# First attention with the keys on the partitions and a rough pass for the maxima, W1 loaded in each expert stage, latent rows placed in two parts

## The chip, the cores and the metric

The kernel runs on one NeuronCore of a Trainium2 chip, as one program. The metric is the device time of one execution in microseconds; the figure of a version is the median of its runs. The engines are TensorE (PE), VectorE (DVE), ScalarE (ACT), GpSimd (POOL) and SyncE (SP, here only the engine that issues transfers). They run side by side and wait for each other by semaphores only.

## The reference

Two sequences of 1024 tokens with 256 values each, all in float32. Six blocks follow each other, each added to x after a layer norm:

```python
x = x + 0.5 * moe(layernorm(x))                  # 16 experts, top 2, 256 -> 512 -> 256, silu
x = x + attention(layernorm(x))                  # 16 heads of 16: see below
x = x + 0.5 * moe(layernorm(x))                  # the same weights again
x = x + 0.5 * lora_ffn(layernorm(x))
x = x + latent_attention(layernorm(x))           # 16 heads, 64 rotary values, latents of 48 and 64
x = x + 0.5 * lora_ffn(layernorm(x))
```

The first attention is the one that the change rewrites:

```python
scores = einsum('bthd,bshd->bhts', q, k) * tril(ones((T, T)))
attn = softmax(scores / T ** 0.5, axis=-1)
out = einsum('bhts,bshd->bthd', attn, v).reshape(B, T, H * Dh)
return out @ Wo
```

The mask multiplies: a later key has the score 0, not minus infinity, and so the weight exp(0 - max). Its part of the result is exp(-max) times the sum of all later values, and the kernel, which computes no scores of later keys, adds that part by itself.

## The kernel before, in words

The stages run one after the other on one core: load, experts 0, first attention, experts 1, a small stage of experts with low rank (lora), the latent attention (mla), lora again, store. x stays in SBUF throughout. Each stage is a block in which every engine has its own list of instructions; nothing is scheduled by a planner, so the order of the work on an engine is the order in which its code is written, and where engines must meet a semaphore is waited for.

**First attention** (`attention_stage`, lines 538 to 1003). A group is 4 heads of one sequence; there are 4 groups in each of 2 sequences, in loops of the hardware. Rows of x are normalised, transposed on PE (L678), and projected by Wqkv (L689) for one group at a time, 8 tiles of 128 tokens. To keep float32 accuracy in one fast pass, the queries and keys are split in a high and a low part (rounded to fp32r, and the rest), which lie side by side in rows QS and KS; PE transposes them (L699) into QT and KT, in 64 rows for each head, so that one matmul with all 128 rows gives high times high, high times low and low times high. A unit is one tile of 128 queries and one head, 32 units in a group. For each: scores with the queries on the partitions (L719), the maximum of each row on DVE (L921, L922 with the mask on the diagonal, L933 for its negative), the exponential on ACT with the negative maximum as the bias of each partition (L850), then a transpose of each 128x128 tile of probabilities on PE (L730), a copy of it from PSUM by ACT (L869), and the values (L740, float32, four heads in four column tiles of 32). An extra column of ones in the values gives the denominator. The parts of later keys come from L750 and L751 (tiles of sums that POOL makes), the rows of the result from DVE (L951 to L967), and after each sequence the output projection (L794, L807). Probabilities of the next units and the projections of the next group are written between, by the tables `steps` and `ahead`.

**Experts** (`moe_stage`). The weights W1 (16 experts, 8.4 MB) and W2 (8.4 MB) lie in SBUF. W1 is loaded once, in experts 0 (L253), and stays there through the first attention; W2 is loaded in both. The normalised rows XN, too, have one place for the experts and, in between, for the attention's rows. PE waits for both weights and then works through the slots of the experts.

**Latent attention** (`mla_stage`). It works on pairs of heads, 8 in each sequence. In a pair PE writes rough scores (L1490, 512 columns each) for the maxima that DVE takes (L1759), then scores with the keys on the partitions (L1509, three passes of high and low parts), the exponentials on ACT (L1648), the values (L1518). The rows of queries and keys of the next pair are projected (L1458, L1465) meanwhile: ACT writes the high parts SH (L1623), DVE the low parts SL (L1753), and SP moves them to their partitions in QH, QL, KH and KL by transfers from SBUF to SBUF, eight for the rotary rows (L1360) and four for the latent ones (L1364), for each half of the tokens. That is `placed`:

```python
def placed(it, buf, half):
    sp.wait_ge(s_hi.handle, s_hi.at(6 * it + 3 * half + 2))
    sp.wait_ge(s_lo.handle, s_lo.at(6 * it + 3 * half + 2))
    for src, q, k in ((SH, QH, KH), (SL, QL, KL)):
        ...
```

POOL fills QH, QL, KH and KL once (L1386, L1390).

## Time and profile before

| | us |
|---|---|
| median of 3 runs | 2616.44 |
| lowest, highest | 2613.11, 2621.42 |
| profiled execution, its own time | 2618.63 |
| its span in the profile | 2616.8 |
| mean granted clock of PE | 0.909 |
| first attention, from its first instruction to its last | 346.5 to 886.9 |
| experts 0 | 18.0 to some 346 |
| experts 1 | 887.1 to some 1215 |
| latent attention | some 1272 to 2540 |

The profile comes from one execution. Times in the timeline count from the start of the span. A matmul's own duration says little about the rate of PE, since matmuls overlap: the step from one start to the next does. The granted clock is a share of full speed (2.4 GHz), so 0.50 is 1.2 GHz.

### The profile page before, as it was taken

The page shows a single profiled execution, that of the slowest core. Times are in us where ns is not written, and L with a number is a line of the kernel's source. Part 1 is how long each engine was busy: PE and PEld are TensorE (multiplying, and loading weights), DVE is VectorE, ACT ScalarE, POOL GpSimd, SP SyncE. Part 2 cuts the span into 40 slices and gives each one's busy share as a digit, 9 for nine tenths or more (in the row PEclk, how much of TensorE's full clock was granted, in tenths as well). Part 3 has the DMA queues.
Part 4 walks back from the last instruction along what each step waited for, and adds up shares of the span by engine and source line. Part 5 has one row for each costly group of instructions (what it writes and reads, how often), then busy time and mean ns, then how long its engine had stood idle before and what let it go on. Part 6 is the DMA issues. An engine that isn't in the chain of part 4 may idle for free. (4 is left out here: it accounts for less than half of the span.)

```text
span 2616.8 us, 40985 instructions
## 1 busy us (share of the span) xinstructions
PE 2141.2 (82%) x11352; PEld 1398.8 (53%) x11353; DVE 1407.2 (54%) x3614; ACT 979.4 (37%) x2011; POOL 755.6 (29%) x480
## 2 busy tenths in 40 slices
PE   4699549997889859972559999999876999999986
PEld 4466336666666646652435555555463555555455
DVE  5222267785778632226445666666335666666525
ACT  1122148885888412212223333333311333333322
POOL 3100320000000130015204555555601555555531
PEclk9999869998999769996758999999976999999998
DMA  7321210000000331222232222212003122112101
GB/s 319 115 62 60 73 40 2 2 2 2 2 2 2 148 109 58 62 62 59 82 73 49 49 49 48 48 45 48 3 12 80 43 49 48 44 47 48 42 1 43
DMA packets 80101, 139.49 MB, mean 53 GB/s; under 512 B 13136, under 2 KB 47440, under 8 KB 78160
## 3 DMA queue, kind: packets, MB, share of 16 engines
q1 hardware_dynamic: 57680, 106.21, 14.6%
q0 software_dynamic: 6144, 16.79, 2.0%
q10 hardware_dynamic: 16128, 14.69, 1.7%
q8 instruction: 72, 1.18, 0.2%
q14 instruction: 77, 0.63, 0.1%
HBM read 60.95 MB, written 27.39 MB: 34 GB/s over the span
## 5 line engine op out<-in xcount | busy, mean ns | idle before, releaser
L1410 POOL TENSOR_TENSOR mla_PS<-mla_PS,mla_PT 128x1024 f32<-128x1024 f32 x192 | 457.4, 2382 | 269.7 <-ACT mla_PT L1648 266.9
L1759 DVE TENSOR_REDUCE mla_MXP<-PS 128x1 f32<-128x512 f32 x512 | 342.4, 689 | 308.0 <-PE PS L1490 303.7
L1648 ACT ACTIVATE mla_PT<-PS 128x1024 f32<-128x1024 f32 x256 | 262.5, 1025 | 467.4 <-PE PS L1509 465.2
L1490 PE MATMUL PS<-mla_KH,mla_QH 128*128 128x512 f32 x512 | 226.7, 484 | 75.1 <-DMA mla_KL<-mla_SL 61.8
L1518 PE MATMUL PS<-mla_PT,mla_CN 128*64 128x512 f32 x1024 | 284.7, 635 | 0.4 <-ACT mla_PT L1648 0.4
L380 DVE COPY moe_HT<-PS 128x512 f32<-128x512 f32 x96 | 66.4, 692 | 319.5 <-PE PS L505 313.4
L1490 PEld LDWEIGHTS PS<-mla_KH,mla_QH 128*128 128x128 f32 x512 | 96.6, 206 | 253.6 <-DVE mla_MXP L1759 133.3
L1509 PE MATMUL PS<-mla_QH,mla_KH 128*128 128x512 f32 x512 | 215.4, 421 | 0.5 <-ACT mla_QH L1635 0.5
L850 ACT ACTIVATE att_PR<-PS,att_NB 128x128 f32<-128x128 f32 (+7 forms) x256 | 193.4, 756 | 53.5 <-DVE att_NB L933 46.8
L1509 PE MATMUL PS<-mla_QL,mla_KH 128*128 128x512 f32 x512 | 205.5, 401 | 0.0
L1509 PE MATMUL PS<-mla_QH,mla_KL 128*128 128x512 f32 x512 | 204.4, 399 | 0.0
L730 PE MATMUL PS<-C,att_PR 128*128 128x128 f32 x1152 | 174.2, 278 | 10.4 <-ACT att_PR L850 6.1
L499 PE MATMUL PS<-W,moe_ST 128*128 x384 | 177.1, 605 | 2.7 <-issue 1.5
L869 ACT COPY att_PT<-PS 128x512 f32<-128x512 f32 (+3 forms) x384 | 173.0, 494 | 11.3 <-PE PS L730 10.6
L513 PE MATMUL PS<-moe_W,moe_HT 128*128 x768 | 173.7, 379 | 0.0
L533 POOL DMA_INDIRECT XN<-slots_out,moe_PO x32 | 32.8, 1026 | 453.5 <-DMA slots_out<-moe_YS 444.3
L921 DVE TENSOR_REDUCE att_MY<-PS 128x1 f32<-128x128 f32 (+6 forms) x224 | 153.4, 685 | 13.0 <-PE PS L719 10.6
L730 PEld LDWEIGHTS PS<-C,att_PR 128*128 128x128 f32 x1152 | 133.4, 141 | 44.6 <-ACT att_PT L869 18.1
L1771 DVE RECIPROCAL PS<-PS 128x128 f32<-128x128 f32 x128 | 108.7, 917 | 79.7 <-PE PS L1525 79.7
L513 PEld LDWEIGHTS PS<-moe_W,moe_HT 128*128 128x128 f32 x768 | 142.2, 190 | 17.3
L719 PE MATMUL PS<-att_KT,att_QT 128*128 128x512 f32 (+1 forms) x384 | 138.6, 423 | 11.5 <-DVE att_KT L903 5.6
L1410 POOL TENSOR_TENSOR mla_PS<-mla_PT 128x1024 f32<-128x1024 f32 x32 | 75.7, 2367 | 248.9 <-ACT mla_PT L1648 248.9
(263 smaller groups left out, 3514.7 us busy)
## 6 DMA issues: line engine op xcount, KB each, us to landing
moe_W<-in_W_dram SPq DMA_DIRECT2D x8, 2048.0 KB, 25.7
moe_XS<-slots_in SPq DMA_DIRECT2D x100, 128.0 KB, 2.0
slots_out<-moe_YS ACTq DMA_DIRECT2D x96, 128.0 KB, 1.7
W<-in_W_dram SPq DMA_DIRECT2D x4, 2048.0 KB, 14.6
mla_QH<-mla_SH SPq DMA_DIRECT2D x64, 128.0 KB, 2.5
mla_KH<-mla_SH SPq DMA_DIRECT2D x64, 128.0 KB, 2.4
mla_QL<-mla_SL SPq DMA_DIRECT2D x64, 128.0 KB, 2.5
mla_KL<-mla_SL SPq DMA_DIRECT2D x64, 128.0 KB, 2.4
```

Source lines behind the costliest of these rows:

```text
L499: ins = pe.matmul(bank(2 + u)[:, :], ST[:, u, k, :], g.W1[:, experts[u], k, :], start=(k == 0), stop=(k == KD - 1))
L513: ins = pe.matmul(bank(6 + u)[:, 0:D], HT[:, u, k, :], W2[:, experts[u], k, :], start=(k == 0), stop=(k == KF - 1))
L730: ins = pe.transpose(bank(4 + c % 2)[:, k * P:(k + 1) * P], PR[:, n % 2, (k0 + k) * P:(k0 + k + 1) * P], ident)
L850: act.activation(PR[:, n % 2, 0:w], scores(n, w), ACT.Exp, bias=NB[:, n:n + 1], scale=SEQ ** -0.5).then_inc(s_p.handle, 1)
L869: act.copy(PT[:, i % 2, h, k0:k0 + nk, :], bank(4 + c % 2)[:, 0:nk * P].rearrange("p (k s) -> p k s", s=P)).then_inc(s_ptc.handle, 1)
L921: dve.tensor_reduce(MY[:, n:n + 1], scores(n, w)[:, 0:i * P], AX_X, ALU.max).then_inc(s_mx.handle, 1)
L1410: pool.tensor_tensor(PS[:, :], PT[:, slot(0), :] if k == 1 else PS[:, :], PT[:, slot(k), :], ALU.add).then_inc(s_ps.handle, 1)
L1490: pe.matmul(bank(piece_bank(n))[:, :], QH[:, buf, h, tile * P:(tile + 1) * P], KH[:, buf, h, c * HB:(c + 1) * HB], start=True, stop=True). ...
L1509: ins = pe.matmul(bank(st_bank(s, h))[:, :], kk[:, buf, h, ks], qq[:, buf, h, qs], start=(n == 0), stop=(n == 2))
L1518: ins = pe.matmul(bank(6)[h * DKVL:(h + 1) * DKVL, :], CN[:, k, 0:DKVL], PT[:, slot(k), h * HB:(h + 1) * HB], start=(k == 0), stop=(k == T ...
L1648: act.activation(PT[:, slot(k), :], banks(st_bank(s, 0), 2)[:, :], ACT.Exp, scale=MLA_SCALE).then_inc(s_p.handle, 1)
L1759: dve.tensor_reduce(MXP[:, n // NPC, c, h, t:t + 1], bank(piece_bank(n))[:, :], AX_X, ALU.max).then_inc(s_mx.handle, 1)
```

## The change

The first attention is written anew, all eight groups one after another without loops of the hardware, in 24 slots for each.

- Queries and keys are projected for a group of four heads and 512 tokens at once (L759, now with the weights as the stationary operand), so that they come out with the heads on the partitions. ACT writes the high parts SH, DVE the low parts SL, and SP moves 16 rows at a time into QT and KT: 24 transfers a group. Row 32 of each head's 64 rows holds the maximum in QT and -1 in KT.
- A rough pass (L774, 32 of the 64 rows, which leave out the low parts of the queries; the mask is added by L777) writes scores with the queries on the partitions in 40 pieces a group; DVE reduces each. The maxima of four tiles are transposed on PE (L785), and ACT copies four single rows into QT.
- The scores proper (L799, 64 rows, with L803 for the mask) have the keys on the partitions and the maximum already subtracted, so the exponential needs no bias and its result goes into the values (L815) without a transpose. The result is copied (ACT), transposed back for four tiles (L823) and finished by DVE and POOL.
- Rows, values and later parts of the second sequence, and the output projection of the first, are written into slots of the loop, through bank 7.
- W1 and XN have a place of their own in each expert stage, and W1 is loaded in both.
- `placed` waits for the high parts, issues their transfers, and then waits for the low parts, for the rotary and for the latent rows.
- Names of semaphores for the loading and storing of x are merged, the constants get nine more columns, Wqkv is split into Wqk and Wv, and the order of the host's arrays follows.

```diff
-                    if rep == 0:
-                        sp.dma_start(g.W1[:, e:e + 4], dram["W1"][:, e:e + 4]).then_inc(g.s_w1.handle, 16)
+                    sp.dma_start(g.W1[:, e:e + 4], dram["W1"][:, e:e + 4]).then_inc(s_w1.handle, 16)
...
-                    def scores_of(it, n, buf, free):
-                        if n == 0:
-                            pe.wait_ge(s_kc.handle, s_kc.at(TB * (it + 1)))
-                        if not free:
-                            pe.wait_ge(s_p.handle, s_p.at(NU * it + scores_read_before(n)))
-                        i, h = n // HG, n % HG
-                        width = (i // 2 + 1) * 2 * P
-                        for c in range(0, width, 512):
-                            w = min(512, width - c)
-                            ins = pe.matmul(bank(sc_bank(n) + c // 512)[:, 0:w], QT[:, h // 2, h % 2, i * P:(i + 1) * P],
-                                            KT[:, buf, h // 2, c:c + w], start=True, stop=True)
-                        ins.then_inc(s_sc.handle, 1)
...
-                    def probs_transposes(it, n, first):
-                        pe.wait_ge(s_p.handle, s_p.at(NU * it + n + 1))
-                        for c in range(first_chunk[n], first_chunk[n + 1]):
-                            _, k0, nk = chunks[c]
-                            if c >= 2 or not first:
-                                pe.wait_ge(s_ptc.handle, s_ptc.at(NC * it + c - 1))
-                            for k in range(nk):
-                                ins = pe.transpose(bank(4 + c % 2)[:, k * P:(k + 1) * P], PR[:, n % 2, (k0 + k) * P:(k0 + k + 1) * P], ident)
-                            ins.then_inc(s_ptp.handle, 1)
...
+                sp.wait_ge(s_fill.handle, s_fill.at(5))
+                for G in range(NG):
+                    if G >= 2:
+                        sp.wait_ge(s_st.handle, s_st.at(NSL * (G - 1)))
+                    for src, s_made, rows in ((SH, s_hi, ((QT, 0, 0), (KT, 64, 0), (QT, 0, 16), (KT, 64, 33))), (SL, s_lo, ((KT, 64, 16), (QT, 0, 33)))):
+                        sp.wait_ge(s_made.handle, s_made.at(2 * (G + 1)))
+                        for h in range(HG):
+                            for dst, at, row in rows:
+                                to = 64 * (h % 2) + row
+                                sp.dma_start(f32(dst[to:to + DH0, G % 2, h // 2, :]), src[at + DH0 * h:at + DH0 * (h + 1), :]).then_inc(s_rows.handle, 16)
+                sp.wait_ge(s_w.handle, s_w.at(48))
...
+                pool.memset(f32(QT[:, :, :, :]), 0.0).then_inc(s_fill.handle, 1)
+                pool.memset(f32(KT[:, :, :, :]), 0.0).then_inc(s_fill.handle, 1)
+                pool.memset(MB[:, :], 0.0).then_inc(s_fill.handle, 1)
+                pool.wait_ge(s_fill.handle, s_fill.at(3))
+                for h in range(2):
+                    pool.memset(f32(KT[64 * h + 32:64 * h + 33, :, :, :]), -1.0).then_inc(s_fill.handle, 1)
+                    pool.wait_ge(s_fill.handle, s_fill.at(4 + h))
+                pool.memset(VV[:, :, :], 0.0).then_inc(s_fill.handle, 1)
+                pool.wait_ge(s_fill.handle, s_fill.at(6))
+                pool.memset(VV[:, :, :].rearrange("p t (h d) -> p (t h) d", d=VW)[:, :, DH0:DH0 + 1], 1.0).then_inc(s_fill.handle, 1)
+
...
+                def rough_scores(H, ns):
+                    for n in ns:
+                        q, t, _, k0, w, hs = pieces[n]
+                        if n == 0:
+                            pe.wait_ge(s_rows.handle, s_rows.at(NROW * (H + 1)))
+                        if NPC * H + n >= 2:
+                            pe.wait_ge(s_mx.handle, s_mx.at(NPC * H + n - 1))
+                        i = 4 * q + t
+                        diag = k0 + w == (i + 1) * P
+                        out = bank(n % 2)[:, 0:len(hs) * w].rearrange("p (h k) -> p h k", k=w)
+                        for m, h in enumerate(hs):
+                            row = slice(64 * (h % 2), 64 * (h % 2) + 32)
+                            ins = pe.matmul(out[:, m, :], QT[row, H % 2, h // 2, i * P:(i + 1) * P], KT[row, H % 2, h // 2, k0:k0 + w], start=(m == 0),
+                                            stop=(not diag and m == len(hs) - 1))
+                        if diag:
+                            ins = pe.matmul(out[:, :, w - P:w], IDR[:, :], bcast(NQ[:, :], 1, len(hs)), start=False, stop=True)
+                        ins.then_inc(s_sh.handle, 1)
...
+                def max_rows(G, q):
+                    n = 2 * G + q
+                    misc(s_nm, 4 * (n + 1))
+                    pe.wait_ge(s_mb.handle, s_mb.at(n + 1))
+                    for t in range(4):
+                        ins = pe.transpose(MISC[:, t * P:(t + 1) * P], MB[:, t:t + P], ident)
+                    ins.then_inc(s_mt.handle, 1)
...
+                def scores_of(G, s):
+                    q, j = key_of(s // 2)
+                    pair = s % 2
+                    if s in (0, TB):
+                        pe.wait_ge(s_nm.handle, s_nm.at(4 * (2 * G + q + 1)))
+                    if NSL * G + s >= 2:
+                        pe.wait_ge(s_p.handle, s_p.at(NSL * G + s - 1))
+                    c0 = columns(q, j)
+                    diag = j >= 4 * q
+                    for hh in range(2):
+                        row = slice(64 * hh, 64 * hh + 64)
+                        ins = pe.matmul(st_banks(s)[:, hh, c0:HB], KT[row, G % 2, pair, j * P:(j + 1) * P], QT[row, G % 2, pair, q * HB + c0:(q + 1) * HB],
+                                        start=True, stop=not diag)
+                    if diag:
+                        for hh in range(2):
+                            ins = pe.matmul(st_banks(s)[:, hh, c0:c0 + P], IDR[:, :], NK[:, :], start=False, stop=True)
+                    ins.then_inc(s_st.handle, 1)
...
+                def values_of(G, kk):
+                    q, j = key_of(kk)
+                    pe.wait_ge(s_p.handle, s_p.at(NSL * G + 2 * kk + 2))
+                    if j == 0:
+                        pe.wait_ge(s_oc.handle, s_oc.at(2 * G + q))
+                    c0 = columns(q, j)
+                    tile, last = TB * (G // NG0) + j, 4 * q + 3
+                    for h in range(HG):
+                        hv = (G % NG0 * HG + h) * VW
+                        ins = pe.matmul(bank(6)[h * VW:(h + 1) * VW, c0:HB], VV[:, tile, hv:hv + VW], PT[:, kk % 2, h, c0:HB], start=(j == 0), stop=(j == last))
+                    ins.then_inc(s_v.handle, 1)
...
+                rough_scores(0, range(NPC0))
+                max_rows(0, 0)
+                rough_scores(0, range(NPC0, begin[0]))
+
+                for G in range(NG):
+                    for s in range(NSL):
+                        H, todo = pieces_at(G, s)
+                        scores_of(G, s)
+                        if s == 6:
+                            max_rows(G, 1)
+                        if s == 17 and G + 1 < NG:
+                            max_rows(G + 1, 0)
+                        rough_scores(H, todo[:1])
+                        if s % 2 == 0 and (s or G):
+                            values_of(G if s else G - 1, s // 2 - 1 if s else NKEY - 1)
+                        rough_scores(H, todo[1:])
+                        if (G, s) in filler:
+                            fill(*filler[G, s])
+                        if s == 4 and G:
+                            out_transposes(G - 1, 1)
+                        if s == 11:
+                            out_transposes(G, 0)
+                        if projected_at(G, s):
+                            K, half = projected_at(G, s)
+                            misc(s_lo, 2 * K + half + 1)
+                            projections(K, half, MISC)
+                values_of(NG - 1, NKEY - 1)
+                out_transposes(NG - 1, 1)
+                for i in range(TB + 1):
...
+                act.wait_ge(s_fill.handle, s_fill.at(7))
...
+                def max_copies(G, q):
+                    n = 2 * G + q
+                    act.wait_ge(s_mt.handle, s_mt.at(n + 1))
+                    for h in range(HG):
+                        row = 64 * (h % 2) + 32
+                        act.copy(QT[row:row + 1, G % 2, h // 2, q * HB:(q + 1) * HB], MISC[VW * h:VW * h + 1, :]).then_inc(s_nm.handle, 1)
...
+                def maxima(H, ns):
+                    for n in ns:
+                        q, t, c, k0, w, hs = pieces[n]
+                        dve.wait_ge(s_sh.handle, s_sh.at(NPC * H + n + 1))
+                        out = MX[:, q, c, hs[0]:hs[-1] + 1:2, t]
+                        dve.tensor_reduce(out, bank(n % 2)[:, 0:len(hs) * w].rearrange("p (h k) -> p h k", k=w), AX_X, ALU.max).then_inc(s_mx.handle, 1)
...
                     def placed(it, buf, half):
                         tok = slice(half * HB, (half + 1) * HB)
-                        sp.wait_ge(s_hi.handle, s_hi.at(6 * it + 3 * half + 2))
-                        sp.wait_ge(s_lo.handle, s_lo.at(6 * it + 3 * half + 2))
-                        for src, q, k in ((SH, QH, KH), (SL, QL, KL)):
+                        for src, q, k, s_made in ((SH, QH, KH, s_hi), (SL, QL, KL, s_lo)):
+                            sp.wait_ge(s_made.handle, s_made.at(6 * it + 3 * half + 2))
                             for h in range(2):
                                 for m, dst in enumerate((q, k)):
                                     i = 32 * (2 * m + h)
                                     sp.dma_start(f32(dst[ROT, buf, h, tok]), src[i:i + 32, 0:2, :]).then_inc(s_kr.handle, 16)
-                        sp.wait_ge(s_lo.handle, s_lo.at(6 * it + 3 * half + 3))
-                        for src, k in ((SH, KH), (SL, KL)):
+                        for src, k, s_made in ((SH, KH, s_hi), (SL, KL, s_lo)):
+                            sp.wait_ge(s_made.handle, s_made.at(6 * it + 3 * half + 3))
                             for h in range(2):
                                 sp.dma_start(f32(k[LAT, buf, h, tok]), src[h * 64:h * 64 + DQL, 2, :]).then_inc(s_kl.handle, 16)
 
@@ -1841,7 +1940,7 @@
 
 
```


**Order of the instructions.** On PE, in the main loop of a group before (L719 scores, L730 transposes of probabilities, L699 transposes of queries and keys, L740 values):

```order
L719 MATMUL PS<-att_KT,att_QT 128x512 [waits att_probs]
L719 MATMUL PS<-att_KT,att_QT 128x256
L728 REGISTER_ALU [waits att_probs]
L730 MATMUL PS<-C,att_PR 128x128 [waits att_probsT_copied]
L730 MATMUL PS<-C,att_PR 128x128 x3
L728 REGISTER_ALU
L730 MATMUL PS<-C,att_PR 128x128 [waits att_probsT_copied]
L694 ISA
L699 MATMUL PS<-C,att_QS 128x128 [waits att_low_parts]
L699 MATMUL PS<-C,att_QS 128x128
L699 MATMUL PS<-C,att_KS 128x128 x2
L740 MATMUL PS<-att_PT,att_VV 32x128 [waits att_out_sum,att_probsT_copied]
```


And now on PE, in slots 17 and 18 of the first group (L799 scores, L803 masks, L785 the rows of maxima, L774 rough scores, L815 values):

```order
L799 MATMUL PS<-att_QT,att_KT 128x512 [waits att_probs]
L799 MATMUL PS<-att_QT,att_KT 128x512
L803 MATMUL PS<-att_NK,att_IDR 128x128 x2
L785 MATMUL PS<-C,att_MB 128x128 [waits att_block_max,att_xnT_copied]
L785 MATMUL PS<-C,att_MB 128x128 x3
L774 MATMUL PS<-att_KT,att_QT 128x512 [waits att_piece_max] x2
L799 MATMUL PS<-att_QT,att_KT 128x384 [waits att_probs]
L799 MATMUL PS<-att_QT,att_KT 128x384
L803 MATMUL PS<-att_NK,att_IDR 128x128 x2
L774 MATMUL PS<-att_KT,att_QT 128x512 [waits att_piece_max]
L815 MATMUL PS<-att_PT,att_VV 32x512 [waits att_probs]
L815 MATMUL PS<-att_PT,att_VV 32x512 x3
```


The runs of equal instructions are gone: between two sets of scores PE now changes from tiles of 64 rows to 128, to 32, to column tiles of 32, and back. Before, only the values had a tile of their own.

On SP, in the latent attention, the transfers of half a pair before:

```order
L1360 DMA mla_QH<-mla_SH 64x1x512 [waits mla_low_parts,mla_high_parts]
L1360 DMA mla_KH<-mla_SH 64x1x512
L1360 DMA mla_QH<-mla_SH 64x1x512
L1360 DMA mla_KH<-mla_SH 64x1x512
L1360 DMA mla_QL<-mla_SL 64x1x512
L1360 DMA mla_KL<-mla_SL 64x1x512
L1360 DMA mla_QL<-mla_SL 64x1x512
L1360 DMA mla_KL<-mla_SL 64x1x512
L1361 REGISTER_ALU
L1364 DMA mla_KH<-mla_SH 48x512 [waits mla_low_parts]
L1364 DMA mla_KH<-mla_SH 48x512
L1364 DMA mla_KL<-mla_SL 48x512 x2
```


And now:

```order
L1459 DMA mla_QH<-mla_SH 64x1x512 [waits mla_high_parts]
L1459 DMA mla_KH<-mla_SH 64x1x512
L1459 DMA mla_QH<-mla_SH 64x1x512
L1459 DMA mla_KH<-mla_SH 64x1x512
L1459 DMA mla_QL<-mla_SL 64x1x512 [waits mla_low_parts]
L1459 DMA mla_KL<-mla_SL 64x1x512
L1459 DMA mla_QL<-mla_SL 64x1x512
L1459 DMA mla_KL<-mla_SL 64x1x512
L1461 REGISTER_ALU
L1463 DMA mla_KH<-mla_SH 48x512 [waits mla_high_parts]
L1463 DMA mla_KH<-mla_SH 48x512
L1463 DMA mla_KL<-mla_SL 48x512 [waits mla_low_parts]
```


The wait for the low parts moved from ahead of the first transfer to ahead of the fifth, and in the latent rows from the first to the third.

## Rows read from the trace of the kernel before

**Rows 1.** Windows: us, each engine's busy time (instructions), granted clock, DMA share, GB/s.

```profile
346.50:886.90 540.40, 472.78 (x4656) 356.09 (x4656) 403.90 (x1561) 418.24 (x1051) 27.34 (x52) 0.97 0.01 4
```

**Rows 2.** The page's costliest groups, three of the attention's.

```profile
L850 ACT ACTIVATE att_PR<-PS,att_NB 128x128 f32<-128x128 f32 (+7 forms) x256 | 193.4, 756 | 53.5 <-DVE att_NB L933 46.8
...
L730 PE MATMUL PS<-C,att_PR 128*128 128x128 f32 x1152 | 174.2, 278 | 10.4 <-ACT att_PR L850 6.1
...
L869 ACT COPY att_PT<-PS 128x512 f32<-128x512 f32 (+3 forms) x384 | 173.0, 494 | 11.3 <-PE PS L730 10.6
```

**Rows 3.** The page's group of L1490, its idle time and what ended it.

```profile
L1490 PE MATMUL PS<-mla_KH,mla_QH 128*128 128x512 f32 x512 | 226.7, 484 | 75.1 <-DMA mla_KL<-mla_SL 61.8
```

**Rows 4.** Timeline of PE in one pair of the latent attention: start, us.

```profile
1547.41 1.03 PE L1518 MATMUL PS<-mla_PT,mla_CN 128*64 128x512 f32 x4
1548.37 0.50 PE L1509 MATMUL PS<-mla_QH,mla_KH 128*128 128x512 f32 x1
...
1549.62 0.40 PE L1509 MATMUL PS<-mla_QH,mla_KL 128*128 128x512 f32 x1
1553.01 0.49 PE L1490 MATMUL PS<-mla_KH,mla_QH 128*128 128x512 f32 x1 [2.99 <-DMA mla_KL<-mla_SL]
```

**Rows 5.** Timeline of ACT, DVE and SP in the same pair.

```profile
1539.68 1.07 ACT L1623 CAST mla_SH<-PS 128x512 fp32r<-128x512 f32 x2
...
1542.27 1.27 DVE L1753 TENSOR_TENSOR mla_SL<-PS,mla_SH 128x512 fp32r<-128x512 f32 x2
...
1543.63 0.60 SPq L1360 DMA_DIRECT2D mla_QH<-mla_SH  x1
...
1548.11 0.60 SPq L1360 DMA_DIRECT2D mla_KL<-mla_SL  x1
1548.81 1.17 SPq L1364 DMA_DIRECT2D mla_KH<-mla_SH  x2
1550.03 1.23 SPq L1364 DMA_DIRECT2D mla_KL<-mla_SL  x2
```

**Rows 6.** Windows of PE alone: us, busy, granted clock, DMA share, GB/s.

```profile
1554.50:1557.50 3.00, 3.00 (x9) 0.50 0.00 0
1749.60:1756.20 6.60, 6.58 (x16) 0.54 0.00 0
```

**Rows 7.** Windows of the experts: both weight loads, then W2 alone.

```profile
18.00:81.00 63.00, 29.94 (x136) 27.84 (x136) 29.66 (x153) 11.17 (x25) 31.68 (x32) 1.00 0.91 367
887.00:947.00 60.00, 29.92 (x136) 27.84 (x136) 29.75 (x153) 11.17 (x25) 31.35 (x32) 0.51 0.65 246
```

**Rows 8.** Timeline of PE, tiles of 128 rows, then of 64.

```profile
1590.73 0.39 PE L1509 MATMUL PS<-mla_QH,mla_KL 128*128 128x512 f32 x1
1590.95 0.40 PE L1490 MATMUL PS<-mla_KH,mla_QH 128*128 128x512 f32 x1
1591.28 0.50 PE L1465 MATMUL PS<-mla_CTH,mla_GH 64*128 64x512 f32 x1
1591.62 0.39 PE L1465 MATMUL PS<-mla_CTL,mla_GH 64*128 64x512 f32 x1
1591.86 0.39 PE L1465 MATMUL PS<-mla_CTH,mla_GL 64*128 64x512 f32 x1
```

**Rows 9.** The page's groups of a float32 matmul and of a reduce.

```profile
L1759 DVE TENSOR_REDUCE mla_MXP<-PS 128x1 f32<-128x512 f32 x512 | 342.4, 689 | 308.0 <-PE PS L1490 303.7
...
L499 PE MATMUL PS<-W,moe_ST 128*128 x384 | 177.1, 605 | 2.7 <-issue 1.5
```

**Rows 10.** Groups by shape: copies of one row, memsets.

```profile
L1635 ACT CAST mla_QH<-PS 1x512 fp32r<-1x512 f32 x64 | 36.8, 575 | 102.6 <-PE PS L1497 101.8
...
L650 POOL MEMSET att_QT<- 128x4096 f32 x1 | 3.5, 3515 | 0.0
...
L1390 POOL MEMSET mla_KL<- 1x4096 f32 x1 | 3.5, 3502 | 0.1
```

**Rows 11.** Timeline of ACT: the first exponential.

```profile
372.66 0.37 ACT L850 ACTIVATE att_PR<-PS,att_NB 128x128 f32<-128x128 f32 x1 [2.19 <-DVE att_NB L933]
```

760 lines of the change are left out of this document (391 added, 369 removed).

## The prediction

> **What bounds the kernel now.** I read the windows by stage first, then the page's costliest groups, then the timeline where PE idles. In the first attention, 346.5 to 886.9, PE is busy 472.8 of 540.4 us at a granted clock of 0.97 [rows 1]. Less some 80 us of beginnings and ends, that is eight groups of heads of 57.6 us each. ACT is busy 418 us and DVE 404 [rows 1]. So PE bounds it, with ACT and DVE not far behind (by their shares, 45 and 43 us of a group). Three groups show what the layout costs: 193.4 us of exponentials and 173.0 us of copies on ACT, and 1152 transposes of probabilities on PE, 174.2 us [rows 2]. The latent attention is bound by PE too, but has a hole in each pair of heads: L1490 sat idle 75.1 us, 61.8 of them until transfers into mla_KL had landed [rows 3]. One case: PE's last matmul starts at 1549.62 and the next at 1553.01 [rows 4]. The SL half was complete on DVE at 1543.54, SP issued its first transfer at 1543.63 although ACT had finished the SH half at 1540.75, and the last of 12 issues ended at 1551.26 [rows 5]. After the hole the granted clock is 0.50 for some 3 us, in 4 of 14 cases 0.54 over 6.6 us [rows 6]. A matmul that takes 0.23 us takes 0.43 there.
>
> **Latent attention.** The total work stays; four SH transfers go before the wait for SL. SP then issues them at about 1540.8 to 1543.4 (pitch 0.64, from 1543.63 to 1548.11 for eight [rows 5]), the SL four from 1543.6 to 1546.2, the latent four to 1548.7. The last landed 1.75 us after its issue ended before (1551.26 to 1553.01), so now at about 1550.4, against 1550.0 where PE runs dry: a hole of 0.4 instead of 3.0 us. What is late next is nothing on SP: its following wait is one pair later. The 14 holes sum to 44.8 us, and the two beginnings of a sequence make up the rest of the 61.8; 2.6 us each is 36. Without a hole the clock should stay up: ten falls of 1.7 us and four of 3.4 are 30 us [rows 6]; I count 28. The two beginnings of a sequence (8.5 us of idle each) save 1.7 each, 3.4. Sum -68 us. Ends: -45 if half the falls stay, -80 if the holes close fully and the clock's loss was larger. I take the value for a hole below 0.5 us, since the landing time is a measured difference.
>
> **W1 again.** Four loads of 2048 KB return to the second experts stage. The first one, with both loads, took 63.0 us from its start to the first slot load, the second, with W2 only, 59.6; DMA share is 0.91 against 0.65 there [rows 7], so the extra 8.4 MB lie beside the router's work mostly. +3.4 us (0 to +6). The merged semaphores of x and the nine more columns of constants cost nothing: they touch the two ends of the program, where one wait takes the place of another.
>
> **First attention.** PE loses the transposes of probabilities, of QS and KS, and gains rough scores and masks. Counted from the order of the program, for all 8 groups, at full clock: an F32R pass over 512 columns starts every 0.23 us [rows 8], one of 384, 256, 128 columns 0.17, 0.11 and 0.11 (no row shows 128 columns alone; between 0.06, a quarter of 0.23, and 0.151, L730's 174.2/1152 [rows 2], which holds waits too). A float32 matmul is two passes, for 512 columns of 0.43 to 0.46 us each (177.1/384 at most [rows 9]).
> - Rough scores L774: 384 matmuls, 192 of 512, 64 of each other width: 69.5 us. Scores L799: the same, 69.5.
> - Masks L777 192 and L803 256: 20.5 + 27.4.
> - Values L815, 96 sets of four column tiles of 32, 48 sets over 512 columns; L1518's pair of column tiles, four passes, gives 0.96 to the next start with one change of tile in it, 0.85 without [rows 4]; 61.9.
> - Projections L759 27.3, transposes (192) 21, values, later values and output L740, L748, L751, L835 41.
>
> Sum 338. The two matmuls of a scores pair lie on different 64 rows. Whether they run together no row shows (L1465 uses the same 64 rows and its passes follow at 0.24 [rows 8]); between 0 and -42 I take -20.
> **Changes of tile size** are what the new order is full of: 920 (to 128 rows 359, to 32 rows 273, to 64 rows 192, to column tiles 96) against some 350 before. From 128 to 64 rows the next start is 0.33 us later instead of 0.23, and the one after that 0.34 too [rows 8]: 0.10 to 0.21 a change. By TensorEngine Tiling (Array Packing) of the Trainium skill, section Key Properties, changing the tiling mode drains TensorE; the trace agrees, 0.10 us or more. The same counting gives 57.6 us for a group of before with 0.175 a change, which is what the trace has, so 0.175: 161 us. PE needs 338 - 20 + 161 = 479 us.
> Of that about 30 us lie in the prologue and 9 in the tail; the loop is 440, 55 a group. Four us a group I add for waits: at slot 6 ACT copies four rows of maxima, 4 x 0.575 = 2.3 us [rows 10], and the scores of slot 8 wait for them, with ACT's full exponentials (1.03 us each) queued behind; DVE's reduces (40 a group, up to 0.69 each [rows 9]) sum to 24 us and hide. Loop 472.
> **Prologue.** ACT now waits for seven fills on POOL before its first copy: two of 4096 elements at 3.5, two of one row at 3.5 (one partition costs what 128 do), one of 8192, 7, and small ones [rows 10]: 22.8 us, to 369.4 (before, the first copy ran at 354.6). Rows, values and projections take to 382, two low parts and 24 transfers at 0.64 (15.4) to 399, 26 rough pieces through DVE with the maxima between to 416.5: 70 us, against 26 before (346.5 to 372.7 [rows 11]). The second sequence has no prologue of its own now; its rows and values are filled into slots of the loop, counted above. The tail is 13. Whole stage 70 + 472 + 13 = 555 against 540: **+15 us**. Ends: -95 and +85, from the price of a change and of a pair, below.
>
> **Sum.** -68 + 3.4 + 15 = -50 us against the profiled execution's 2618.6, which is 2.2 above the median 2616.4: **2569 us**. ACT and DVE, 45 and 43 us of a group before, come to about 28 and 30, which buys nothing as long as PE is the bound.
>
> **Rivals.** (a) *Changes of tile are cheap and pairs run together.* At 0.10 a change, -69, and another -22 for scores and rough pieces on different rows: attention 464, total 2478. For it: L1518's two column tiles do overlap, four passes of 0.43 in 0.96 [rows 4]. Against it: both the 0.33 and the 0.34 are there for one change [rows 8]. The page TensorE: Matmul & The Clock Gate of the Trainium skill, its section on small K, says that matmuls on different row groups run concurrently, starting within 4 ns of each other; no row here shows it for rows. By that rule alone the pairs would give the other -22 and a total of 2547.
> (b) *The change of tile decides, on the slow side.* Place: PE between each rough piece, its mask, the scores and the values. If a change costs 0.25, as where drain, exposed weight load and restart add (0.10 + 0.11 + some), 920 x 0.075 = +69: attention 624, total 2638, slower than before. It decides from about 0.24 a change. For: the second 0.34. Against: the group of before, calibrated at 0.175.
> (c) *The hole stays.* If another transfer or DVE's low part ends the wait, and the clock falls all the same, MLA gives 20 and not 68: total 2617, no change. Against: SP is idle before 1543.6, ACT's part is ready 2.9 us before [rows 5].
>
> **Numbers.** Forecast case (2530 to 2605) 0.52; (a) 0.19, of it half above 2500; (b) 0.17; (c) 0.12, two thirds within the bound. 0.3%, 8 us, is about what a measurement of this kernel can tell. Faster by more: 0.52 + 0.19 + 0.03 + 0.01 from (b)'s lower end = 0.75; same 0.08; slower 0.17. Range 2495 to 2630; it leaves out (a)'s cheaper half and (b)'s dearer half.
>
> **What would show it.** In the new profile: the idle time of L1490's successor near 15 us instead of 75, and the clock of a pair's start at 1.00; the starts of a scores matmul after a rough mask 0.30 to 0.40 us after that mask; PE busy over 85% of a group of 59 us; the first exponential 70 us after the stage's start; ACT's busy share in the stage about half. A group of under 50 us says (a), one over 65 says (b). Holes of 3 us in the latent attention say (c). I would be wrong altogether if PE had long waits in the loop, for the rows of maxima or the exponentials, of more than 4 us a group.

## The result, and the profile after

| | before | after |
|---|---|---|
| median, us | 2617.91 (4 runs, 2613.11 to 2621.42) | 2742.27 (4 runs, 2741.94 to 2749.36) |
| ratio, 95% interval | | 1.0483 (1.0458 to 1.0507): slower |
| span of the profiled execution | 2616.8 | 2739.9 |
| mean granted clock of PE | 0.909 | 0.837 |
| first attention | 346.5 to 886.9: 540.4 | 346.5 to 1074.5: 728.0 |
| experts 1, start to first slot load | 887.13 to 946.74: 59.6 | 1074.53 to 1135.00: 60.5 |

The forecast was 2569 us, the range 2495 to 2630. The kernel became 124 us slower. The attention alone lost 187.6 us; the rest of the program gave some 64 back, nearly all in the latent attention, which takes 1227.1 us from its first instruction to its last where it took 1291.7.

First the page of the changed kernel: the line of the granted clock in 40 slices, and a group of instructions. L1589 is what L1490 was [rows 3].

```profile
PEclk9999765566657766699866599999997699999998
...
L1589 PE MATMUL PS<-mla_KH,mla_QH 128*128 128x512 f32 x512 | 218.0, 465 | 35.7 <-DMA mla_KL<-mla_SL 22.4
```

The idle time of the rough scores of the latent attention that transfers end has gone from 61.8 us [rows 3] to 22.4, of which 7.6 each are the two beginnings of a sequence; the 14 holes of 3 us are now 0.41 to 0.49 us, one 1.38. That part did what it was meant to. The clock line has the news: between the sixth and the sixteenth slice, where the attention lies, PE is granted 0.5 to 0.7 of full speed. The windows say it for the stage and for the main loop from the first exponential to the last:

```profile
346.50:1074.50 728.00, 665.72 (x2428) 332.59 (x2428) 252.53 (x469) 238.52 (x371) 62.77 (x75) 0.64 0.11 19
431.70:1059.70 628.00, 601.34 (x2232) 289.39 (x2232) 212.70 (x392) 219.97 (x329) 32.57 (x57) 0.64 0.11 18
```

PE is busy 601 of 628 us, so it hardly waits, and the granted clock is 0.64, where it was 0.97 before [rows 1], with more waiting (472.8 of 540.4 us busy). ACT and DVE work a third of the time. Time multiplied by the granted clock gives 402 us for the loop; I call that the product below. It is less than what the loop would take at full clock, as e5 shows. A timeline of PE in the second group shows how a slot reads at 1.2 GHz:

```profile
560.16 0.79 PE L799 MATMUL PS<-att_QT,att_KT 64*128 64x512 f32 x2
560.88 0.69 PE L734 MATMUL PS<-C,att_XNS 128*128 128x128 f32 x2
...
562.23 1.93 PE L815 MATMUL PS<-att_PT,att_VV 128*32 128x512 f32 x8
564.09 0.79 PE L799 MATMUL PS<-att_QT,att_KT 64*128 64x512 f32 x2
```

and the same kinds of instruction in the sixth group, in a stretch at full clock:

```profile
838.95 0.44 PE L799 MATMUL PS<-att_QT,att_KT 64*128 64x384 f32 x2
839.32 0.44 PE L803 MATMUL PS<-att_NK,att_IDR 128*128 128x128 f32 x2
...
840.22 1.07 PE L815 MATMUL PS<-att_PT,att_VV 128*32 128x512 f32 x8
841.22 0.50 PE L774 MATMUL PS<-att_KT,att_QT 32*128 32x512 f32 x1
```

Two scores matmuls of 384 columns and the change to the masks take 0.37 us there (838.95 to 839.32); two of 512 and a change take 0.72 in the slow stretch (560.16 to 560.88), and 0.43 at full clock in e2 below. The values over 512 columns take 1.00 against 1.86. The clock is at one level or the other and moves between them within a group, as windows of 3 us in the second group show:

```profile
561.00:564.00 3.00, 3.00 (x12) 0.50 0.00 0
567.00:570.00 3.00, 3.00 (x18) 1.00 0.00 0
573.00:576.00 3.00, 3.00 (x17) 1.00 0.00 0
579.00:582.00 3.00, 3.00 (x13) 0.50 0.00 0
```

PE has no idle time in any of the four.

### The profile page after: what moved, and what is told of

Read it like the earlier page. It is cut to its first block and busy times, and to the rows that moved or that the text cites. A ratio compares the mean times of both kernels' runs of the same rounds, so it can differ in the third digit from the quotient of the medians.

```text
span 2739.9 us, 32413 instructions
## 1 busy us (share of the span) xinstructions
PE 2306.4 (84%) x9124; PEld 1362.4 (50%) x9125; DVE 1254.9 (46%) x2522; ACT 800.0 (29%) x1331; POOL 791.2 (29%) x503
## 5 line engine op out<-in xcount | busy, mean ns | idle before, releaser
L1044 DVE TENSOR_REDUCE att_MX<-PS 128x1 f32<-128x512 f32 (+3 forms) x320 | 200.1, 636 | 342.7 <-PE PS L777 249.7
L1617 PE MATMUL PS<-mla_PT,mla_CN 128*64 128x512 f32 x1024 | 274.6, 615 | 0.4 <-ACT mla_PT L1747 0.4
L1589 PE MATMUL PS<-mla_KH,mla_QH 128*128 128x512 f32 x512 | 218.0, 465 | 35.7 <-DMA mla_KL<-mla_SL 22.4
L960 ACT ACTIVATE att_PT<-PS 128x1024 f32<-128x1024 f32 (+1 forms) x192 | 155.6, 812 | 292.9 <-PE PS L803 233.4
L1589 PEld LDWEIGHTS PS<-mla_KH,mla_QH 128*128 128x128 f32 x512 | 92.5, 196 | 204.8 <-DVE mla_MXP L1858 133.3
L774 PE MATMUL PS<-att_KT,att_QT 32*128 32x512 f32 (+3 forms) x384 | 185.1, 568 | 10.1 <-DVE att_MX L1044 8.2
L698 POOL TENSOR_TENSOR att_AO<-att_F,att_RC 128x256 f32<-128x256 f32 x16 | 9.9, 621 | 607.2 <-DVE att_RC L1069 607.2
L534 POOL DMA_INDIRECT XN<-slots_out,moe_PO x32 | 32.5, 1016 | 454.3 <-DMA slots_out<-moe_YS 445.1
L1608 PEld LDWEIGHTS PS<-mla_QH,mla_KH 128*128 128x128 f32 x512 | 96.6, 189 | 81.8 <-issue 35.4
L774 PEld LDWEIGHTS PS<-att_KT,att_QT 32*128 32x128 f32 x384 | 78.8, 239 | 115.1 <-DVE att_MX L1044 53.9
```

Source lines behind the costliest of these rows:

```text
L774: ins = pe.matmul(out[:, m, :], QT[row, H % 2, h // 2, i * P:(i + 1) * P], KT[row, H % 2, h // 2, k0:k0 + w], start=(m == 0), stop=(not di ...
L960: act.activation(PT[:, kk % 2, 2 * pair:2 * pair + 2, c0:HB], st_banks(s)[:, :, c0:HB], ACT.Exp, scale=SEQ ** -0.5).then_inc(s_p.handle, 1)
L1044: dve.tensor_reduce(out, bank(n % 2)[:, 0:len(hs) * w].rearrange("p (h k) -> p h k", k=w), AX_X, ALU.max).then_inc(s_mx.handle, 1)
L1589: pe.matmul(bank(piece_bank(n))[:, :], QH[:, buf, h, tile * P:(tile + 1) * P], KH[:, buf, h, c * HB:(c + 1) * HB], start=True, stop=True). ...
L1608: ins = pe.matmul(bank(st_bank(s, h))[:, :], kk[:, buf, h, ks], qq[:, buf, h, qs], start=(n == 0), stop=(n == 2))
L1617: ins = pe.matmul(bank(6)[h * DKVL:(h + 1) * DKVL, :], CN[:, k, 0:DKVL], PT[:, slot(k), h * HB:(h + 1) * HB], start=(k == 0), stop=(k == T ...
```

## The experiments

Eleven kernels ran. Theory A says that the kinds of tile in the new order bring the clock down. Theory B says that changes of tile are dearer than I took them for and the clock falls with idle time only; under e8 it stands for something else, that the changes themselves bring the clock down. Theory C, from e5 on, looks for the cause outside PE. The latent attention is looked at by itself first. Where I give a number of changes of tile, it is counted from the matmul records of the trace: 919 in the stage of the changed kernel.

**e1_two_part.** The kernel before, with the transfers of the latent attention in two parts:

```diff
-                        sp.wait_ge(s_hi.handle, s_hi.at(6 * it + 3 * half + 2))
-                        sp.wait_ge(s_lo.handle, s_lo.at(6 * it + 3 * half + 2))
-                        for src, q, k in ((SH, QH, KH), (SL, QL, KL)):
+                        for src, q, k, s_made in ((SH, QH, KH, s_hi), (SL, QL, KL, s_lo)):
+                            sp.wait_ge(s_made.handle, s_made.at(6 * it + 3 * half + 2))
```

> The kernel before, with the transfers of the latent attention in two parts and nothing else. If this part gives what the prediction said, the holes before L1490 fall from 45 to about 6 us and the clock no longer falls after them: 2618 - 68 = 2550 us. If only the holes shrink and the clock falls all the same, 2618 - 39 = about 2579. If another wait takes over, over 2600.

Measured: 2556.47 us, ratio 0.9763 (0.9747 to 0.9779), 61.9 us less than the runs of before beside it. Its page has

```profile
L1489 PE MATMUL PS<-mla_KH,mla_QH 128*128 128x512 f32 x512 | 218.6, 467 | 38.2 <-DMA mla_KL<-mla_SL 24.9
```

36.9 us fewer of waiting for mla_KL, and the window of a pair (1386 to 1452) that had a clock of 0.97 in the kernel before now has 1.00. The other 25 us are what is left over, and I put them down to the clock: the mean over the whole span went from 0.909 to 0.918, which is some 29 us less of lost clock. The change's small half is good for 2.4% on its own.

**e2_micro.** A program that only loads x, lets PE run stretches of one kind of matmul from a copy of it, and stores x; all stages are left out.

```diff
+                for i in range(80):
+                    r = slice(64 * (i % 2), 64 * (i % 2) + 64)
+                    pe.matmul(nb(i % 2), A[r, 0:P], A[r, 512:1024], start=True, stop=True)
+                warm()
...
+                for i in range(24):
+                    for h in range(2):
+                        pe.matmul(nb(h), A[64 * h:64 * h + 64, 0:P], A[64 * h:64 * h + 64, 512:1024], start=True, stop=True)
+                    for h in range(2):
+                        pe.matmul(nb()[:, 0:P], A[:, P:2 * P], A[:, 1024:1024 + P], start=True, stop=True)
```

> Only x is loaded and stored; between them PE runs stretches of matmuls of one kind, each after a stretch of 44 F32R matmuls with all 128 rows (0.23 us each at full clock). Theory A, the kind of tile sets the clock: in the stretches with tiles of 32 rows, and perhaps of 64, the granted clock falls to 0.50 although PE never waits, and it stays 1.00 in those with 128 rows. Theory B, only idle time lowers the clock and the changes of tile are dear: the clock is 1.00 everywhere, and a period of two 64-row matmuls over 512 columns and two of 128 rows over 128 columns takes 1.3 us or more instead of 0.7 to 0.9. Also: if two row tiles run side by side, 80 matmuls on alternating 64 rows take 80 x 0.12 = 9 us, if not 18.

The timeline of PE: 80 matmuls on alternating 64 rows (L1977) up to the next stretch; the period of two 64-row matmuls (L1996) and two masks (L1998); and 100 matmuls of 128 columns (L2015):

```profile
40.24 9.38 PE L1977 MATMUL PS<-mi_A 64*128 64x512 f32 x80
49.56 10.29 PE L1972 MATMUL PS<-mi_A 128*128 128x512 f32 x44
...
173.92 0.50 PE L1996 MATMUL PS<-mi_A 64*128 64x512 f32 x2
174.35 0.44 PE L1998 MATMUL PS<-mi_A 128*128 128x128 f32 x2
174.72 0.49 PE L1996 MATMUL PS<-mi_A 64*128 64x512 f32 x2
...
308.48 11.28 PE L2015 MATMUL PS<-mi_A 128*128 128x128 f32 x100
319.59 10.25 PE L1972 MATMUL PS<-mi_A 128*128 128x512 f32 x44
```

Eighty matmuls take 9.32 us, 0.117 each: two row tiles do run side by side, which no row of the kernel before could show. The period with two changes of tile is 0.80 us. Of it 0.23 is the pair and 2 x 0.111 the masks (11.11 us for 100), which leaves 0.35, or some 0.17 a change: the figure of the prediction. For a dearer change theory B has no ground left at full clock. The windows of the stretches, all of them without idle time of PE:

```profile
40.20:49.50 9.30, 9.30 (x81) 1.00 0.00 0
59.80:75.80 16.00, 16.00 (x71) 1.00 0.00 0
86.10:95.30 9.20, 9.20 (x81) 1.00 0.01 2
105.60:132.80 27.20, 27.20 (x71) 0.56 0.00 1
144.70:163.60 18.90, 18.90 (x177) 1.00 0.01 2
173.90:193.00 19.10, 19.10 (x97) 1.00 0.00 1
203.20:240.40 37.20, 37.20 (x73) 0.56 0.00 0
253.00:273.00 20.00, 20.00 (x142) 1.00 0.00 1
```

Full speed holds for pairs of 64 rows (40.2), for 64 rows alone (59.8), for 32-row tiles in turn at two places (86.1), column tiles (144.7), pairs with masks (173.9) and pairs with column tiles (253.0). It falls to 0.50 during single 32-row matmuls (105.6), and during single 32-row matmuls with a mask each (203.2): these two windows average 0.56. Part of theory A holds, but the pair with its masks doesn't lower the clock here.

**e3_rough64.** The rough scores on 64 rows, no tile of 32 rows left:

```diff
-                            row = slice(64 * (h % 2), 64 * (h % 2) + 32)
+                            row = slice(64 * (h % 2), 64 * (h % 2) + 64)
```

> The changed kernel with the rough scores on 64 rows instead of 32, and the row of maxima set to zero by two transfers more in each group from the third on. The tiles of 32 rows are gone, and PE changes tiles some 650 times instead of 920. Theory A with the 32 rows as the cause: granted clock of the attention over 0.85 instead of 0.65, total about 2600 or less. Theory A with any row tile as the cause: about as the changed kernel, 2700 to 2740. Theory B: 270 changes of 0.2 to 0.35 us less, 2650 to 2690, at the same clock.

Measured: 2700.9 us (1.0314, 1.0259 to 1.037), from two runs of 2713.1 and 2688.7 that differ in their mean granted clock too, 0.843 and 0.851; in the profiled one, the 2713.1, the loop takes 601.5 us at 0.66. The 32 rows as such are not the cause, or not alone. The expectation had the changes wrong: the trace has 842 in the stage, 77 fewer than the changed kernel and not 270, since a rough piece is rarely next to the scores. So e3 says little about the price of a change.

**e4_rows128.** QT for four heads, zero in the other head's rows, so that all score matmuls use 128 rows:

```diff
-                            row = slice(64 * (h % 2), 64 * (h % 2) + 32)
-                            ins = pe.matmul(out[:, m, :], QT[row, H % 2, h // 2, i * P:(i + 1) * P], KT[row, H % 2, h // 2, k0:k0 + w], start=(m == 0),
+                            ins = pe.matmul(out[:, m, :], QT[:, H % 2, h, i * P:(i + 1) * P], KT[:, H % 2, h // 2, k0:k0 + w], start=(m == 0),
...
-                        row = slice(64 * hh, 64 * hh + 64)
-                        ins = pe.matmul(st_banks(s)[:, hh, c0:HB], KT[row, G % 2, pair, j * P:(j + 1) * P], QT[row, G % 2, pair, q * HB + c0:(q + 1) * HB],
+                        ins = pe.matmul(st_banks(s)[:, hh, c0:HB], KT[:, G % 2, pair, j * P:(j + 1) * P], QT[:, G % 2, 2 * pair + hh, q * HB + c0:(q + 1) * HB],
```

> The changed kernel with QT widened to four heads, zero in the other head's rows, so that rough scores and scores use all 128 rows as in the kernel before; 192 changes of tile (for the values) instead of 920; the pairs no longer run side by side. Theory A: the clock stays over 0.95 in the loop, a group takes 46 to 52 us, the stage 480 to 520, total 2490 to 2530. Theory B (dear changes, clock a side effect): the same time saved by fewer changes, 700 x 0.3 = 210 us, so a total near 2530 too, but then with a clock of 0.65 still in the stage and periods that don't scale; if neither, 2700 or more.

Measured: 2524.86 us, ratio 0.9641 (0.9625 to 0.9657): faster than both kernels, and 31.6 us faster than e1. The loop, from first to last exponential:

```profile
429.20:845.10 415.90, 373.19 (x2232) 240.54 (x2231) 207.80 (x392) 218.35 (x329) 32.66 (x57) 0.94 0.16 28
```

The clock is 0.94, and the loop 212 us shorter. The products, 391 us here and 402 in the changed kernel, lie close together, but they count waits as work and halve everything at the low level. By the estimate under e5 the loop would take 395 us at full clock here and 440 in the changed kernel. So some 45 of the 212 us come from less work: 192 changes of tile in the stage instead of 919, less what the pairs lose that no longer run side by side. The other 167 are the clock. The 0.94 answers theory B, which expected 0.65.

**e5_micro2.** More stretches without waits, from full clock and from 0.50 (all other work left out again).

> Again only x is loaded and stored. First, from full clock: one 64-row matmul and a mask of 128 rows in turn; a pair of 32-row matmuls and two masks in turn; the slot of the changed kernel (pair of scores on 64 rows, two masks, rough piece of 32 rows, mask, four column tiles of float32, rough piece, mask). Then the same kinds and the plain ones after a stretch of 40 single 32-row matmuls that has brought the clock to 0.50. Theory A (the share of the array's rows in use decides): the slot's clock falls to 0.50 from full clock, or at least never comes back from 0.50, while pairs, column tiles and 128 rows do come back within 7 us. Theory C (the fall comes from something outside PE, such as waits for the other engines in the loop): every stretch except single 32-row ones comes back to 1.00, the slot's too.

The windows, in their order: 64 rows alone with a mask; a 32-row pair with two masks; the changed kernel's slot, these from full clock; then, from 0.50: 64-row pairs; pairs with two masks; column tiles; float32 matmuls of 128 rows; the slot; the slot with rough pieces of 64 rows.

```profile
41.00:78.50 37.50, 37.50 (x73) 0.56 0.00 0
90.90:124.20 33.30, 33.30 (x113) 0.59 0.00 0
136.00:164.30 28.30, 28.30 (x145) 1.00 0.00 1
192.00:203.00 11.00, 11.00 (x81) 0.82 0.00 0
231.90:253.10 21.20, 21.20 (x65) 0.50 0.00 0
281.60:293.40 11.80, 11.80 (x97) 0.87 0.00 1
363.80:373.30 9.50, 9.50 (x20) 0.86 0.01 2
402.40:434.90 32.50, 32.50 (x97) 0.50 0.00 1
463.40:495.90 32.50, 32.50 (x97) 0.50 0.00 1
```

Two things come out. A single 64-row matmul and a mask in turn lose the clock too (0.56), although single 64-row matmuls alone kept it in e2. And the slot of the changed kernel has no clock of its own: it ran 28 us at 1.00 when it came from 1.00, a period of 3.16 us, and 32 us at 0.50 when it came from 0.50, a period of 5.4 us (32.5 / 6). So did the pair with masks (1.00 in e2, 0.50 here). Column tiles, 64-row pairs by themselves and matmuls with 128 rows come back within their stretch. Theory C is out: no other engine works here, and the slot stays at 0.50. Theory A's weaker form, "never comes back from 0.50", came out for the slot, but for the pair with masks too, and that the slot also keeps full clock for 28 us was in neither. I call it theory D, the mix holds whichever level it finds.

The two periods also give a conversion. 5.4 / 3.16 is 1.71 and not 2. From e2's numbers the slot's matmuls take 2.0 us at full clock (pair 0.23, four masks 0.44, two rough pieces 0.46, column tiles 0.86), so its seven changes of tile take 1.16 us, 0.17 each. A matmul of 0.23 us takes 0.43 at half clock, so the matmuls take 3.7 to 4.0 us there, and a change some 0.20 to 0.24: it doesn't double. So I estimate a loop at full clock by its time at 0.50, which is twice the missing share of the clock, divided by 1.71. For the changed kernel that is 0.72 x 628 = 452 us at 0.50, 264 at full clock, and with the other 176 us a loop of 440.

**e6_rough128 and e7_scores128.** Each undoes one half of e4: in e6 the rough scores have 128 rows and the scores 64-row pairs, in e7 the scores have 128 and the rough scores 32.

> The rough scores on 128 rows as in e4, the scores proper still as two 64-row matmuls side by side. Theory A with the single rough pieces as the cause: clock over 0.9 in the loop and scores 35 us shorter than in e4, so 2500 to 2530 in all, in spite of some 380 changes of tile more than e4 (at 0.175, 67 us: 2555). If the 64-row pairs with their masks are the cause: clock 0.6 to 0.8 and 2650 to 2720.

> The scores proper on 128 rows as in e4, the rough scores on 32 rows as in the changed kernel, so single 32-row tiles between full ones. Theory A: clock below 0.85 in the loop, 2600 to 2700. If only 64-row pairs lower it: clock over 0.9, 2540 to 2570 with the added changes of tile.

Measured: e6 2554.16 us (0.9757, 0.9712 to 0.9801), e7 2655.32 (1.0143, 1.0092 to 1.0194). The loops of e3, e7 and e6 from first to last exponential, PE alone:

```profile
431.80:1033.30 601.50, 571.97 (x2232) 0.66 0.11 19
434.90:979.80 544.90, 509.56 (x2232) 0.77 0.13 21
429.50:877.20 447.70, 411.15 (x2232) 0.89 0.15 26
```

With all versions side by side, the estimate at full clock made as under e5, the changes counted over the stage:

| version | rough scores, scores | loop, us | granted clock | product | at full clock (estimate) | changes of tile |
|---|---|---|---|---|---|---|
| after | 32, 64 | 628.0 | 0.64 | 402 | 440 | 919 |
| e3 | 64, 64 | 601.5 | 0.66 | 397 | 432 | 842 |
| e7 | 32, 128 | 544.9 | 0.77 | 420 | 441 | 652 |
| e6 | 128, 64 | 447.7 | 0.89 | 398 | 407 | 536 |
| e4 | 128, 128 | 415.9 | 0.94 | 391 | 395 | 192 |

The rough pieces, issued singly with a mask behind each, carry most of the loss: widening them alone gives 180 us (after to e6). Widening the scores alone gives 83 (after to e7), and 32 where the rough scores are wide already (e6 to e4), so the two are not simply added. At full clock the loops would differ by 46 us at most, where they differ by 212.

**e8_no_masks.** The masks of rough scores and scores are left out, so later keys in a diagonal tile count as earlier ones.

```diff
-                        diag = k0 + w == (i + 1) * P
+                        diag = False
```

> The changed kernel without the masks of rough scores and scores (448 small matmuls; later keys within a diagonal tile are counted as if they were earlier). At full clock they and the changes of tile around them are 48 us of passes and some 90 us of changes. Theory A: the masks are work on all 128 rows, so without them the clock is no better, 0.60 to 0.65, and the time falls to about 2740 - 140/0.65 = 2530 at most, 2600 if the clock gets worse. Theory B (changes of tile lower the clock): clock over 0.9, below 2500.

Measured in one run: 2600.59 us; the loop:

```profile
423.40:921.60 498.20, 442.29 (x1802) 0.68 0.14 23
```

At full clock that would be 366 us, 74 less than the changed kernel, and not the 140 that I wrote. The trace has 569 changes of tile where I had counted on some 500 fewer than 919, so at 0.175 they are 61 us and not 90; and PE now waits 56 us in the loop and not 27. With masks of 48 us, 48 + 61 - 29 = 80 is near the 74. The clock is still 0.68. e6, with nearly as many changes (536), has 0.89. So the number of changes by itself doesn't set the clock.

**e9_burst_first and e10_burst_each.** If the mix holds whichever level it finds, raising the clock once should help for long. Useless full matmuls go ahead of the first scores, once in e9, in each group in e10:

```diff
+                    if s == 0 and G == 0:
+                        for i in range(36):
+                            pe.matmul(bank(2), KT[:, G % 2, 0, 0:P], QT[:, G % 2, 0, 0:HB], start=True, stop=True)
```

> The changed kernel with 36 matmuls more, 128 rows and 512 columns each, once ahead of the first scores of the first group (8 us at full clock, 16 at half; their results are written over). Theory D, the clock has two stable levels for this mix of tiles (it holds 1.00 if it comes from 1.00 and stays at 0.50 if it comes from 0.50): the loop begins at 1.00 instead of 0.50 and stays there until PE's first wait or lean stretch, so the first group is 10 to 25 us shorter, and the total 2720 to 2740, as later dips bring the low level back. Theory A' (the mix itself pulls the clock down in any case): the clock is back at 0.50 within 7 us of the burst, and the total is 2750 to 2760.

> The same burst ahead of the first scores of each of the 8 groups: 8 x 8 to 16 = 64 to 130 us of useless work. Theory D: each group then runs its first part, until slot 6 or so, at 1.00 instead of 0.50, which gives back 8 x 12 to 25 us; total 2680 to 2790 with a granted clock of the loop over 0.8. Theory A': clock of the loop as before apart from the bursts, total 2810 to 2870.

Measured: e9 2759.54 us in one run, e10 2832.89 (1.082, 1.0789 to 1.0852), with a clock of 0.65 in its loop where theory D wanted over 0.8. Windows of PE in e9, and rows of its timeline:

```profile
425.00:431.00 6.00, 5.74 (x12) 0.50 0.00 0
431.00:436.00 5.00, 5.00 (x19) 0.79 0.00 0
446.00:451.00 5.00, 5.00 (x23) 1.00 0.23 35
456.00:461.00 5.00, 5.00 (x18) 0.50 0.60 101
476.00:481.00 5.00, 5.00 (x28) 1.00 0.00 0
```

```profile
430.31 9.74 PE L797 MATMUL PS<-att_QT,att_KT 128*128 128x512 f32 x36
439.98 0.50 PE L802 MATMUL PS<-att_QT,att_KT 64*128 64x512 f32 x2
...
452.45 0.49 PE L774 MATMUL PS<-att_KT,att_QT 32*128 32x512 f32 x1 [0.67 <-DVE att_MX L1047]
...
453.24 0.38 PE L802 MATMUL PS<-att_QT,att_KT 64*128 64x256 f32 x2
453.56 0.69 PE L806 MATMUL PS<-att_NK,att_IDR 128*128 128x128 f32 x2
```

The burst raises the clock, and the real loop then runs 13 us at full speed (439.98 to 453.56): slot 0 to 3. In them PE runs four single rough pieces with a mask each, between 443.9 and 449, and later waits 0.67 us for a reduce, up to 452.45. At 453.56, five matmuls behind that wait, it is back at 0.50; at 476 it is up again by itself. Against the changed kernel, e9 costs 17 us and e10 91, more than the bursts give: both totals are what was expected of a mix that pulls the clock down in any case. So D describes the steady slot of e5, but the loop doesn't keep a high clock as that slot did; raising it by added work doesn't pay here. Which ended the full speed at 453.56, the wait or the lean pieces around it, this run can't tell; in e2 and e5 a lean stretch alone was enough.

**e11_fills_first.** e4 with POOL's fill of the values ahead of the others and ACT waiting for that one only:

> The version of e4 (all 128 rows), with POOL's fill of the values first, and ACT waiting for that alone, and that only ahead of its first copy of values; the fills of QT and KT and their two rows then run beside the transposes and projections. The first copy came 20 us after the stage's start; now it comes 8 us after, and everything up to the first rough piece moves 12 to 14 us ahead: 2524.9 - 13 = 2512. Rival: the transfers into QT and KT wait for the fills, which now end last, and 0 to 5 us are won.

Measured: 2522.32 us (0.9634, 0.9611 to 0.9658), 2.5 less than e4, and the runs of the two overlap (2519.6 to 2525.7 here, 2524.0 to 2526.9 in e4). That is the rival's 0 to 5 us, for another reason: the fills end at 375.1 and the first transfer is issued at 387.2, so no transfer waited for them. DVE's and POOL's timelines:

```profile
352.79 11.38 DVE L140 TENSOR_SCALAR att_XNS<-X,MV,RS 128x256 f32<-128x256 f32 x2
...
376.13 0.41 DVE L140 TENSOR_SCALAR att_XNS<-X,MV,RS 128x256 f32<-128x256 f32 x1 [0.53 <-PE PS L738]
...
349.65 6.92 POOL L658 MEMSET att_VV<- 128x8192 f32 x1 [8.06 <-SPq L116]
...
357.05 6.97 POOL L661 MEMSET att_QT<- 128x8192 f32 x1
```

DVE's first two normalised tiles (XNS) last 3.9 and 7.5 us. They end at 356.7 and 364.2, each 0.15 us behind the end of a fill of POOL, of VV and of QT; at 376.1, with no fill running, a tile takes 0.41 us. The waits for the fill are gone from ACT, and have turned up inside DVE's instructions.

## Why the prediction was wrong

- **The step that failed** is the sum of the first attention, "Counted from the order of the program, for all 8 groups, at full clock". That PE would be granted full clock was taken over from the stage before, with its 0.97 [rows 1], and none of the rivals for this stage had the clock in it. The loop was put at 472 us. It took 628 at a granted clock of 0.64; at full clock it would have taken some 440 (estimate, from e5's two periods), so the clock cost some 188 us.
- **What the total would have been.** With the clock of before, 0.97, the loop would take some 451 us by the same estimate, and the kernel 2742 - (628 - 451) = 2565, where the forecast was 2569. That is close partly by luck: a loop forecast some 20 us too long stands against a prologue and tail forecast 17 us too short and a latent attention that gave 6 us less than forecast.
- **A change of tile at 0.175 us** was right at full clock (0.17, e2 and e5). Rival (b), the only one on the slow side, named the right sign for a wrong reason: a price of 0.25. It gave 2638.
- **Pairs side by side**, taken at -20 between 0 and -42: two row tiles overlap fully (0.117 us for each of them, e2). The page TensorE: Matmul & The Clock Gate of the Trainium skill says in its part on packing small matmuls that those on different row groups run concurrently; e2's number agrees. My weight on it was too low. Those 22 us, and waits of less than the 4 us a group that I added (PE idles 27 us of 628, 3.3 a group), bring 472 to 445, near the 440 above.
- **The latent attention**, -68: e1 shows -61.9, of it 36.9 in holes (39 forecast) and 25 for the clock (28 forecast). The mechanism and the size held.
- **W1**, +3.4: experts 1 takes 60.5 us to its first slot load instead of 59.6, so +0.9. The transfers lie beside the router's work.
- **Prologue**, 70 us: the first exponential comes at 431.7, so 85. The steps up to the transfers came as written (first copy at 371.2, SH at 384.4, last transfer issued at 401.4, against 369.4, 382 and 399). Then 26 rough pieces, put at the pace of DVE (17.5 us), took 28.5, with PE busy for 26.0 of them at a granted clock of 0.52. Tail 15 (13).
- The checks that the prediction named worked in part: "PE busy over 85% of a group" came out (96%), with a group of 78 us. "One over 65 says (b)" was a bad test, since it would have taken any slow group for dear changes.

What stays open: what exactly in the lean stretches, the few rows, the 128-column masks or the gaps at a change, brings the clock down. The stretches of e2 and e5, one run each, name kinds that do and kinds that don't; they don't separate the parts. Waits of this size alone don't do it: the kernel before waited more at 0.97. Nor does the number of changes alone (e6 against e8).

## What to carry to other kernels

When a change replaces full matmuls by tiles of 32 or 64 rows, by small masks and by changes between them, read the granted clock as a term of its own: count the work at full speed, and then ask at which of the two levels it will run. Padding to 128 rows with zeros gave up pairs side by side here, some 35 us by the prediction's sum (half of 69.5), and made the loop 212 us shorter all the same, some 167 of them by the clock. A stretch of the real mix, run in a small program once from full clock and once from half, would have shown before the kernel was written that it can stay at half. And part a change: its smallest piece, four transfers ahead of a wait, was worth 2.4% alone.

## What the runs showed of the hardware that was not expected

- A granted clock of 0.50 with PE never idle: single 32-row matmuls (0.56 over 27 us), single 32-row or 64-row matmuls with a mask each (0.56), a 32-row pair with two masks (0.59).
- The same sequence of instructions at either level for as long as it ran: 28 us at 1.00 or 32 us at 0.50.
- A change of tile costs 0.17 us at full clock, and some 0.20 to 0.24 at half (estimate, from e5's periods of 3.16 and 5.4 us).
- A normalisation on DVE that takes 0.41 us lasted 3.9 and 7.5 us while POOL filled SBUF (two in 11.38 us beside two fills of 6.9 us), and ended with the fill. So the fills ahead of this stage delay it even where nobody waits for them by a semaphore.
